# Two float16 parts of the normalised rows in the projection, and transposing DMAs for the experts' rows

## The chip, the cores and the metric

The kernel runs on one core of one Trainium2 chip. The metric is the device time of one execution in microseconds (us), lower is better. Five engines work side by side and meet at semaphores: PE (matmuls), ACT, DVE and POOL (elementwise work), and SP, which here does nothing but issue DMAs, in one order, from one queue. The kernel before takes 1036.85 us (median of 3 runs, 1036.43 to 1039.17).

## The reference, cut to what matters

```python
x = L0_attn_X                                   # (2, 2048, 256) float32
xn = (x - mean) / sqrt(var + 1e-5)              # layernorm over the last axis
qkv = xn @ Wqkv                                 # 16 heads of 16, rope on q and k
attn = softmax(causal(q @ k.T / 4)) @ v         # each head
out_a = attn @ Wout + bout
p = softmax(xn @ gate_w.T + gate_b)             # 8 experts and 2 null ones
w, e = top_k(p, 2)                              # null ones masked, the rest renormalised
out_f = sum_k w[k] * (xn @ expert_w[e[k]] + expert_b[e[k]])
return x + out_a + out_f
```

## The kernel before

Float32 products are made of float16 parts: a value is a high part plus a low part, and three float16 products (high by high, high by low, low by high) replace one float32 product. So everything that PE multiplies has to be split somewhere.

**Projection** (`project`, until about 135 us). 4096 rows are taken in 8 steps s of 512 rows (chunk j, batch b, s = 2j + b). In a step:
- DVE takes the statistics (L480, L484) and forms `rstd` and `less` (L489, L491).
- ACT writes the normalised rows to `xn` as float32 (`normal_x`, L405) for step s + 2, near the end of its step s.
- PE turns them by 8 transposes against a float32 identity into `psT` (`transposes`, L709). It does so for step s + 1 between the second and the third of a step's four `queries` products, and then computes `values` (L717).
- ACT copies `psT` to float16 as the high part (`high_x`, L388). DVE subtracts to get the low part (`low_x`, L498).
- DVE multiplies each product by the rope tables (`rope`, L559). POOL combines the halves (L356, L358). ACT and then POOL or DVE split the result (`high` L413, `low` L345, `split` L564).
- SP stores `xn` as float32 rows to `norm_scratch` (L257), and the parts of q, k and v.

ACT's order in a step matters below: `high(s-1, 2)`, `high(s-1, 3)`, `high_x(s+1)`, `high(s, 0)`, `high(s, 1)`, `copy_v`, `normal_x(s+2)`, `high_e(s)`. So the cast that POOL's second `low` of a step waits for stands behind the next `normal_x`.

**Attention and experts** (`attend`, about 135 to 1000 us). Eight groups g of four heads. What each engine does in a group is written out in a string, `PE_ORDER`: `s` is a score matmul, `p` the product of one block of probabilities with V, digits are matmuls for the row maxima (reduced on DVE), `m` and `o` small transposes, `x` and `y` expert work. All engines walk the same string, each doing its own share in that order. Items other than `s` and `p` take turns in the two slots of `psP`.

Groups 2 to 5 are of the kind "experts". The token rows, sorted by expert, form 36 pairs of 128-row tiles, 9 per group. For pair n:
- POOL fetches its rows by indirect DMA (`fetch`, L1130) and splits them into float16 parts (`split`, L1141 and L1143).
- `x`: PE turns them by 8 transposes (`turn_x`, L1478). ACT copies the high half (L1231), DVE the low half (L1303) to `xT`.
- `y`: PE multiplies by the experts' weights (`expert`, 12 matmuls of 256 columns at L1494 and two for the bias at L1496). ACT copies the result out (L1234). SP waits for that copy, stores it (`store_e`, L1050) and loads the weights of pair n + 2 (`load_e`, two register reads of the expert's number and four DMAs, L1044 and L1046).

Between these, SP also issues the loads of heads for group g + 2 (L74, 24 DMAs, and L1027) and the small stores of row maxima (`store_m`, L1038), each at its place in the same order.

**Output** (`output`, the last 40 us): transposes, the Wout product and the sums.

Of the kernel before, what the change touches and what calls it, by code (L numbers as in the profile page):

```python
# [27 lines left out]
P = 128  # L28
# [29 lines left out]
ONE = 1  # L58
# [23 lines left out]
def project(nc, x, wqk, wvg, we, be, bout, gb, cos, sin, qk_s, v_s, we_s, be_s, xd, ys, acc, xn, escale, idx, unscale, etab, bo,  # L82
            hot, ge, eye, later, identf, identh, lane, number, at, Qs, Ks):
    with ExitStack() as ctx:
# [36 lines left out]
        less = [sb(f"less{i}", [P, CT]) for i in range(2)]  # L121
        vst = [sb(f"vst{i}", [P, CT, HEADS, VW]) for i in range(2)]
# [24 lines left out]
        past = sb("past", [P, MTILES, EXPERTS])  # L147
# [15 lines left out]
        xn_ok = sem("xn_ok")  # L163
# [37 lines left out]
        tables = sem("tables")  # L201

# [9 lines left out]
        def _(sp):  # L212
# [61 lines left out]
        def _(pool):  # L274
# [3 lines left out]

            def step(ins):
                steps[0] += 1  # L280
                return ins.then_inc(pool_step, 1)

            def stepped():
# [7 lines left out]
                                    pattern=[[-1, P]], channel_multiplier=1).then_inc(const, 1)  # L291
            for b in range(NB):
                nc.gpsimd.memset(vst[b][:, :, :, :], 1.0).then_inc(const, 1)
# [25 lines left out]
            pool.sem_inc(const, 1)  # L319

# [3 lines left out]
            nc.gpsimd.memset(identh[:, :], 0.0).then_inc(pool_b, 1)  # L324
            pool.wait_ge(pool_b, ONE + 4)
# [11 lines left out]
            for unit in (identf, identh):  # L337
                nc.gpsimd.affine_select(out=unit[:, :], in_=unit[:, :], compare_op=ALU.not_equal, fill=1.0, base=0,
                                        pattern=[[-1, P]], channel_multiplier=1).then_inc(const_b, 1)
            pool.wait_ge(const_b, ONE + 4 * SIDES + 2)  # L340
# [6 lines left out]
            def body(j):  # L347
                if j == 1:
                    pool.wait_ge(trig_in[1], ONE + 32)
                for b in range(NB):  # L350
                    s = 2 * j + b
                    for k0 in range(0, QKT, 2):
# [7 lines left out]
                        low(s, k0)  # L360

# [17 lines left out]
        def _(act):  # L379
# [21 lines left out]
            def normal_x(s, j, b):  # L401
                act.wait_ge(less_ok, ONE + s + 1)
                for t in range(CT):
# [1328 lines left out]
```

## Time and profile before

| | us |
|---|---|
| median of 3 runs | 1036.85 |
| span of the profiled execution | 1039.8 |
| projection, 0 to 135 | 135 |
| groups 0 and 1, 135 to 366 | 231 |
| groups 2 to 5, with the experts, 366 to 813 | 447 |
| groups 6 and 7, 813 to 1000 | 187 |
| output | 39.8 |

| engine | busy us, share of the span |
|---|---|
| PE | 926.0 (89%) |
| DVE | 863.4 (83%) |
| ACT | 714.7 (69%) |
| POOL | 462.6 (44%) |

The profile is of one execution; its span is 3 us above the median of the runs. A row of the timeline gives the start, the duration, the engine, the line and the tiles, and in brackets how long the engine sat idle before it and what ended that. Rows for `SPq` are the issuing of a DMA by SP, not the transfer. All tiles of the experts' stage are cut from one big tensor, so the trace calls each of them `xn`.

### The profile page before, as it was taken

To read this page: it belongs to the slowest core of one execution; us is meant where nothing else is said; L and a number is where in the kernel's file an instruction comes from. 1 tells how busy PE (TensorE), PEld (TensorE's weight loads), DVE (VectorE), ACT (ScalarE), POOL (GpSimd) and SP (SyncE) were. 2 spreads that over 40 slices of the span, in tenths; PEclk is the share of its full clock that TensorE was granted. 3 is DMA by queue.
4 is the path that set the end of the run, shared out by engine and by line. 5 is a ranking of instruction groups with operands and counts; after the bars stand their busy time and mean duration, and the time that the engine had idled before them with its cause. 6 is when DMAs were issued, how large, how long until landed. Compare 5 with 4: busy or idle time off the path is not lost. (4 is left out here: it accounts for less than half of the span.)

```text
span 1039.8 us, 22117 instructions
## 1 busy us (share of the span) xinstructions
PE 926.0 (89%) x7874; PEld 388.5 (37%) x7874; DVE 863.4 (83%) x1132; ACT 714.7 (69%) x1542; POOL 462.6 (44%) x588
## 2 busy tenths in 40 slices
PE   3888446999999999999999999999999799999978
PEld 1554312232433334344434433344334333333257
DVE  6999789899899977987797787878797599995856
ACT  3556201788788777876787677867887588789922
POOL 4677568565102234253814564262422255345510
PEclk9999655999999999999999999999999899999989
DMA  9767710301100334054314442255514322012113
GB/s 322 267 240 270 244 44 17 96 3 52 53 2 21 94 113 124 26 155 141 110 42 132 122 136 82 62 155 134 123 34 132 87 58 62 22 57 63 47 41 122
DMA packets 82085, 106.65 MB, mean 103 GB/s; under 512 B 10000, under 2 KB 59064, under 8 KB 80952
## 3 DMA queue, kind: packets, MB, share of 16 engines
q1 hardware_dynamic: 74488, 85.83, 26.0%
q0 software_dynamic: 6528, 17.83, 6.7%
q10 hardware_dynamic: 960, 1.57, 0.5%
q8 instruction: 64, 1.05, 0.4%
q14 instruction: 45, 0.37, 0.1%
HBM read 67.37 MB, written 37.50 MB: 101 GB/s over the span
## 5 line engine op out<-in xcount | busy, mean ns | idle before, releaser
L1268 DVE TENSOR_REDUCE blk<-psP 128x2 f32<-128x1024 f32 (+2 forms) x576 | 639.9, 1161 | 103.5 <-PE psP L1422 43.8
L1213 ACT ACTIVATE probs<-psS 128x512 f32<-128x512 f32 (+3 forms) x1280 | 588.5, 541 | 194.0 <-PE psS L1462 174.4
L1462 PE MATMUL psS<-Qs,Ks 50*128 50x512 f16 (+3 forms) x1280 | 322.8, 355 | 12.6 <-ACT probs L1213 9.2
L1422 PE MATMUL psP<-Ks,Qs 48*128 48x512 f16 (+3 forms) x1280 | 284.2, 365 | 34.8 <-DVE blk L1268 21.9
L1517 PE MATMUL psO<-probs,Vs 128*32 128x512 f32 (+3 forms) x2560 | 305.3, 553 | 10.0 <-POOL probs L1107 8.9
L1107 POOL TENSOR_SCALAR_AFFINE_SELECT probs<-probs 128x512 f32<-128x512 f32 x128 | 88.1, 688 | 356.6 <-ACT probs L1213 341.0
L1462 PEld LDWEIGHTS psS<-Qs,Ks 50*128 50x128 f16 x1280 | 92.8, 94 | 241.8 <-ACT probs L1213 149.1
L1422 PEld LDWEIGHTS psP<-Ks,Qs 48*128 48x128 f16 x1280 | 75.5, 95 | 151.4 <-DVE blk L1268 100.7
L1425 PE MATMUL psP<-later,eye 64*128 64x128 bf16 x1024 | 90.3, 223 | 0.0
L1517 PEld LDWEIGHTS psO<-probs,Vs 128*32 128x32 f32 x2560 | 52.4, 109 | 92.1 <-issue 68.8
L1130 POOL DMA_INDIRECT xn<-norm_scratch,ids x72 | 69.4, 963 | 20.7 <-issue 11.4
L1425 PEld LDWEIGHTS psP<-later,eye 64*128 64x128 bf16 x1024 | 71.8, 99 | 16.4 <-issue 2.1
L1122 POOL TENSOR_SCALAR xn<-lane,at 128x128 f16<-128x128 f32 x64 | 38.5, 601 | 44.9 <-ACT probs L1213 23.8
L1494 PE MATMUL psP<-xn 128*128 128x256 f16 x432 | 57.4, 273 | 0.8 <-DVE xn L1303 0.8
L717 PE MATMUL psQ<-xp,wqp 128*128 128x512 f16 x192 | 47.3, 393 | 10.6 <-DVE turn L559 6.1
L1117 POOL DMA_INDIRECT xn<-expert_scratch,idx x32 | 30.3, 946 | 39.8 <-ACT probs L1213 21.0
L1494 PEld LDWEIGHTS psP<-xn 128*128 128x128 f16 x432 | 39.3, 98 | 21.6 <-DVE blk L1268 9.9
L1143 POOL TENSOR_TENSOR xn<-xn 128x512 f16<-128x512 f32 x36 | 41.6, 1155 | 3.0
L559 DVE TENSOR_TENSOR turn<-psQ,trig 128x1024 f32<-128x1024 f32 x32 | 38.4, 1218 | 2.6 <-DVE part L564 1.8
L1234 ACT COPY xn<-psP 128x512 f32<-128x512 f32 x36 | 21.1, 585 | 26.9 <-PE psP L1496 26.9
L1125 POOL TENSOR_SCALAR xn<-lane,at,number 128x76 f16<-128x76 f32 x64 | 39.3, 614 | 0.0
L356 POOL TENSOR_TENSOR turn<-turn 128x512 f32<-128x512 f32 x16 | 24.0, 1500 | 23.0 <-DVE turn L559 22.7
(171 smaller groups left out, 744.0 us busy)
## 6 DMA issues: line engine op xcount, KB each, us to landing
xn<-we_scratch SPq DMA_DIRECT2D x72, 256.0 KB
expert_scratch<-xn SPq DMA_DIRECT2D x36, 256.0 KB
v_scratch<-vst SPq DMA_DIRECT2D x8, 1024.0 KB, 4.0
qk_scratch<-part SPq DMA_DIRECT2D x32, 256.0 KB, 4.0
Vs<-v_scratch SPq DMA_DIRECT2D x16, 512.0 KB, 4.3
Qs<-qk_scratch SPq DMA_DIRECT2D x168, 32.0 KB
Ks<-qk_scratch SPq DMA_DIRECT2D x168, 32.0 KB
acc<-x SPq DMA_DIRECT2D x8, 512.0 KB, 9.1
```

Of the source, the lines that this page charges most:

```text
L717: ins = pe.matmul(out, lhs(x, w, k), rhs(x, w, k), start=(n == 0), stop=(n == len(todo) - 1))
L1107: nc.gpsimd.affine_select(out=v, in_=v, compare_op=ALU.is_ge, fill=0.0, base=0, pattern=[[0, HG], [1, P]], channel_multiplier=-1).then_inc ...
L1125: nc.gpsimd.tensor_scalar(at_tile[:, n, :], lane[:, 0:MTILES], at[:, 0, n:n + 1], number[:, t:t + 1], ALU.is_equal, ALU.mult).then_inc(lis ...
L1130: nc.gpsimd.indirect_dma_start(out=xt[n % 2][:, t, :], out_offset=None, in_=xd[:, :], in_offset=bass.IndirectOffsetOnAxis(ap=ids[:, 2 * n ...
L1143: nc.gpsimd.tensor_tensor(xs[n % 2][:, 1, :], rows, xs[n % 2][:, 0, :], ALU.subtract).then_inc(x_split, 1)
L1213: nc.scalar.activation(probs[u % NPR][:, h, q0:CH], psS[:, n % SB, q0:CH], ACT.Exp, scale=exp_scale).then_inc(s_read[n % SB], 1)
L1268: nc.vector.tensor_reduce(out, src, AX.X, ALU.max).then_inc(item_ok[slot], 1)
L1422: ins = pe.matmul(psP[:, slot, at:at + w], Qs[r][rows, qt // CT, p, t * P:(t + 1) * P], Ks[r][rows, kc, p, 0:w], start=True, stop=True)
L1425: ins = pe.matmul(psP[:, slot, at + w - P:at + w], eye[all_rows, i, :], later[all_rows, i, :], start=False, stop=True, skip_group_check=True)
L1462: pe.matmul(psS[:, n % SB, q0:CH], Ks[r][rows, kt // CT, p, kt % CT * P:(kt % CT + 1) * P], Qs[r][rows, c, p, q0:CH], start=True, stop=Tru ...
L1494: pe.matmul(psP[:, slot, t * D:(t + 1) * D], xT[buf][:, w0, at_k:at_k + P], wt[2 * buf + t][:, of:of + D], start=(n == 0), stop=False)
L1517: ins = pe.matmul(psO[h * VW:(h + 1) * VW, q0:CH], Vs[r][:, kt, h * VW:(h + 1) * VW], probs[u % NPR][:, h, q0:CH], start=(kt == 0), stop=e ...
```

## The change

In the projection the normalised rows go to a float32 buffer `xf`; ACT casts them to the high part, POOL subtracts to get the low part (`low_rows`), and both lie side by side in `xrows`, in the place of `xn`. PE turns the float16 parts, 16 transposes for 8; ACT and DVE copy one half of `psT` each. The scratch holds both parts, 1024 bytes a row as before. In the experts' stage POOL no longer splits, PE no longer turns; SP issues two transposing DMAs a pair (`turn_x`) behind the store and the loads of the pair before. `x` is struck from the order, and nothing else in it is moved. `fetch(n+2)` now waits on POOL for the turning of pair n.

```diff
+            def low_rows(s):
+                j, b = divmod(s, NB)
+                of = slice(b * TT + j * CT, b * TT + (j + 1) * CT)
+                pool.wait_ge(rh_ok, ONE + s + 1)
+                nc.gpsimd.tensor_tensor(xrows[:, of, 1, :], xf[b][:, :, :], xrows[:, of, 0, :], ALU.subtract).then_inc(rl_ok, 1)
...
+            low_rows(0)
+            low_rows(1)
...
                         low(s, k0)
+                    if s + 2 < NB * CHUNKS:
+                        low_rows(s + 2)
...
             def high_x(s, b):
-                for k in range(KC):
-                    act.wait_ge(xT_ps, ONE + KC * s + k + 1)
-                    nc.scalar.copy(xp[b][:, 0, k, :], psT[:, k, :]).then_inc(xh_ok, 1)
+                act.wait_ge(xT_ps, ONE + 2 * s + 1)
+                nc.scalar.copy(xp[b][:, 0, :, :].rearrange("p k n -> p (k n)"), psT[:, 0, :].bitcast(F16)).then_inc(xh_ok, 1)
...
             def normal_x(s, j, b):
...
-                    ins = nc.scalar.activation(xn[:, tile, :], acc[:, tile, :], ACT.Identity, bias=less[b][:, t:t + 1],
+                    ins = nc.scalar.activation(xf[b][:, t, :], acc[:, tile, :], ACT.Identity, bias=less[b][:, t:t + 1],
                                                scale=rstd[b][:, t:t + 1])
-                ins.then_inc(xn_ok, 1)
+                ins.then_inc(xf_ok, 1)
+                act.wait_ge(xf_ok, ONE + s + 1)
+                nc.scalar.copy(xrows[:, j * CT + b * TT:(j + 1) * CT + b * TT, 0, :], xf[b][:, :, :]).then_inc(rh_ok, 1)
...
             def low_x(s, b):
-                for k in range(KC):
-                    dve.wait_ge(xh_ok, ONE + KC * s + k + 1)
-                    nc.vector.tensor_tensor(xp[b][:, 1, k, :], psT[:, k, :], xp[b][:, 0, k, :], ALU.subtract
-                                            ).then_inc(xl_ok, 1)
+                dve.wait_ge(xT_ps, ONE + 2 * s + 2)
+                nc.vector.tensor_copy(xp[b][:, 1, :, :].rearrange("p k n -> p (k n)"), psT[:, 1, :].bitcast(F16)
+                                      ).then_inc(xl_ok, 1)
...
             def transposes(s, j, b):
-                pe.wait_ge(xn_ok, ONE + s + 1)
-                pe.wait_ge(xl_ok, ONE + KC * s)
-                for k in range(KC):
-                    for t in range(CT):
-                        ins = pe.transpose(psT[:, k, t * P:(t + 1) * P], xn[:, j * CT + b * TT + t, k * P:(k + 1) * P],
-                                           ident[:, :])
+                pe.wait_ge(rl_ok, ONE + s + 1)
+                pe.wait_ge(xh_ok, ONE + s)
+                pe.wait_ge(xl_ok, ONE + s)
+                for w in range(2):
+                    for k in range(KC):
+                        for t in range(CT):
+                            ins = pe.transpose(psT[:, w, :].bitcast(F16)[:, k * CH + t * P:k * CH + (t + 1) * P],
+                                               xrows[:, j * CT + b * TT + t, w, k * P:(k + 1) * P], identh[:, :])
                     ins.then_inc(xT_ps, 1)
...
+            def turn_x(n):
+                sp.wait_ge(x_got[n % 2], 16 * 2 * (n // 2 + 1))
+                for t in range(2):
+                    sp.dma_start_transpose(xT[n % 2].rearrange("p w (k t n) -> p (w k) t n", k=KC, t=2)[:, :, t, :],
+                                           xt[n % 2][:, t, :]).then_inc(x_turned[n % 2], 16)
...
                         store_e(buf, EG * (g - 2) + x[1])
                         if EG * (g - 2) + x[1] + 2 < MTILES_USED // 2:
                             load_e(buf, EG * (g - 2) + x[1] + 2)
+                        if EG * (g - 2) + x[1] + 1 < MTILES_USED // 2:
+                            turn_x(EG * (g - 2) + x[1] + 1)
...
-            def split(n):
-                pool.wait_ge(x_got[n % 2], 16 * 2 * (n // 2 + 1))
...
-                    elif x[0] == "x":
+                    elif x[0] == "y":
                         n = EG * (g - 2) + x[1]
-                        turned[n] = slot_of(m), uses(g, m)
-                        if n + 1 < MTILES_USED // 2:
-                            split(n + 1)
+                        if n + 2 < MTILES_USED // 2:
+                            pool.wait_ge(x_turned[n % 2], 16 * 2 * (n // 2 + 1))
+                            fetch(n + 2)
...
                         elif x[0] == "y":
                             buf, before = pair_of(g, x[1])
+                            pe.wait_ge(x_turned[buf], 16 * 2 * (before + 1))
                             pe.wait_ge(e_in[buf], ONE + 16 * LOADS_E * (before + 1))
```

On ACT, in the projection, from one `normal_x` to the `high_x` after it, this stands before:

```order
L405 ACTIVATE xn<-acc,less,rstd 128x256 x4
L437 ACTIVATE wep<-we_sb,wscale 128x512
L413 CAST part<-turn 128x512 x2
L388 CAST xp<-psT 128x512 x2
L413 CAST part<-turn 128x512
```

and this now:

```order
L427 ACTIVATE xf<-acc,less,rstd 128x256 x4
L431 CAST xn<-xf 128x4x256
L461 ACTIVATE wep<-we_sb,wscale 128x512
L437 CAST part<-turn 128x512 x2
L407 COPY xp<-psT 128x1024
L437 CAST part<-turn 128x512
```

The cast of 1024 elements is new, ahead of the casts of `part` that POOL waits for; two copies have become one.

On POOL, one step of the projection now (L374 and L376 are the sums, L363 is `low`, L291 is `low_rows`):

```order
L374 TENSOR_TENSOR turn<-turn 128x512
L376 TENSOR_TENSOR turn<-turn 128x512
L363 TENSOR_TENSOR part<-turn,part 128x512
L374 TENSOR_TENSOR turn<-turn 128x512
L376 TENSOR_TENSOR turn<-turn 128x512
L363 TENSOR_TENSOR part<-turn,part 128x512
L291 TENSOR_TENSOR xn<-xf,xn 128x4x256
```

Before, the same six rows stood there without the seventh. It stands behind the second `low`.

On SP, in group 2, from the last load of one pair to the store of the next (pairs 4 and 5), with the loads of heads between, now:

```order
L1066 TENSOR_LOAD etab
L1066 ISA x2
L1067 ISA
L1067 DMA xn<-we_scratch 128x1024
L1069 ISA
L1069 DMA xn<-be_scratch 3x256
L1076 DMA_TRANSPOSE xn<-xn 128x4x128 x2
L74 DMA Qs0<-qk_scratch 8x2x1024 x12
L74 DMA Ks0<-qk_scratch 8x2x1024 x12
L1050 DMA Vs0<-v_scratch 128x8x128
L1080 DMA expert_scratch<-xn 128x2x256
```

The row L1076 is new. It turns pair 5, and the turning of pair 6 stands behind everything that is shown below it and the loads after that.

## Rows read from the trace of the kernel before

**Rows 1.** Windows by stage: us, busy per engine (instructions), PEclk, DMA share, GB/s.

```profile
0.00:135.00 135.00, 85.03 (x522) 52.12 (x522) 114.33 (x208) 62.50 (x126) 83.34 (x90) 0.92 0.74 259
272.00:366.00 94.00, 90.56 (x866) 32.67 (x864) 86.05 (x103) 75.06 (x165) 18.99 (x28) 1.00 0.17 48
...
366.00:813.00 447.00, 428.01 (x3932) 178.16 (x3931) 361.78 (x420) 339.87 (x726) 185.81 (x231) 0.99 0.37 106
```

**Rows 2.** Timeline of one projection step: start, duration, engine, line.

```profile
57.54 2.07 ACT L405 ACTIVATE xn<-acc,less,rstd 128x256 f32<-128x256 f32 x4
...
59.50 0.71 ACT L437 ACTIVATE wep<-we_sb,wscale 128x512 f16<-128x512 f32 x1
59.66 1.09 PE L709 MATMUL psT<-ident,xn 128*128 128x128 f32 x8 [1.10 <-ACT xn L405]
60.12 1.13 ACT L413 CAST part<-turn 128x512 f16<-128x512 f32 x2
60.59 2.75 PE L717 MATMUL psQ<-xp,wqp 128*128 128x512 f16 x12
60.80 1.16 POOL L345 TENSOR_TENSOR part<-turn,part 128x512 f16<-128x512 f32 x1 [0.65 <-ACT part L413]
...
62.44 1.28 DVE L498 TENSOR_TENSOR xp<-psT,xp 128x512 f16<-128x512 f32 x2
...
63.63 1.21 DVE L559 TENSOR_TENSOR turn<-psQ,trig 128x1024 f32<-128x1024 f32 x1
...
68.94 1.58 ACT L405 ACTIVATE xn<-acc,less,rstd 128x256 f32<-128x256 f32 x3
```

**Rows 3.** Groups of instructions by shape: busy us, mean ns | idle before.

```profile
L1143 POOL TENSOR_TENSOR xn<-xn 128x512 f16<-128x512 f32 x36 | 41.6, 1155 | 3.0
...
L1478 PE MATMUL psP<-identh,xn 128*128 128x128 f16 x288 | 22.4, 221 | 3.1 <-DVE blk L1268 2.1 <-ACT xn L1234 0.3 <-issue 0.3
...
L421 ACT ACTIVATE wqp<-wqk_sb,wscale 128x1024 f16<-128x1024 f32 x1 | 1.1, 1147 | 1.1 <-DVE wscale L512 1.1
```

**Rows 4.** Timeline of PE, ACT and SP around the first pairs of group 2.

```profile
377.11 0.83 PE L1494 MATMUL psP<-xn 128*128 128x256 f16 x6
...
378.85 0.59 ACT L1234 COPY xn<-psP 128x512 f32<-128x512 f32 x1 [0.91 <-PE psP L1496]
391.46 0.59 ACT L1234 COPY xn<-psP 128x512 f32<-128x512 f32 x1 [0.71 <-PE psP L1496]
398.57 0.58 ACT L1234 COPY xn<-psP 128x512 f32<-128x512 f32 x1 [0.80 <-PE psP L1496]
405.96 0.58 ACT L1234 COPY xn<-psP 128x512 f32<-128x512 f32 x1 [0.83 <-PE psP L1496]
...
383.36 0.31 SPq L1046 DMA_DIRECT2D xn<-be_scratch  x1
```

**Rows 5.** Timeline of SP and ACT around pairs 4 to 6 of group 2.

```profile
443.58 4.05 SPq L74 DMA_DIRECT2D Qs<-qk_scratch  x12
...
457.42 0.30 SPq L1046 DMA_DIRECT2D xn<-be_scratch  x1
...
445.61 0.58 ACT L1234 COPY xn<-psP 128x512 f32<-128x512 f32 x1 [0.77 <-PE psP L1496]
457.32 0.58 ACT L1234 COPY xn<-psP 128x512 f32<-128x512 f32 x1 [0.53 <-PE psP L1496]
```

**Rows 6.** DMA issues: tiles, engine, count, KB each, median us from issue to landing.

```profile
qk_scratch<-part SPq DMA_DIRECT2D x32, 256.0 KB, 4.0
...
we_scratch<-wep SPq DMA_DIRECT2D x8, 256.0 KB, 2.2
...
trig<-sin SPq DMA_DIRECT2D x1, 768.0 KB, 9.8
```

**Rows 7.** Windows on PE around its long idle stretch: us, busy (instructions), PEclk.

```profile
108.00:110.00 2.00, 0.59 (x6) 1.00 0.61 215
110.00:112.00 2.00, 0.00 (x0) 0.71 1.04 366
```

More of the change, by code:

```diff
@@ L121, in project @@
         less = [sb(f"less{i}", [P, CT]) for i in range(2)]
+        xf = [sb(f"xf{i}", [P, CT, D]) for i in range(2)]
+        xrows = xn[:, :, :].rearrange("p t d -> p (t d)").bitcast(F16).rearrange("p (t w d) -> p t w d", w=2, d=D)
         vst = [sb(f"vst{i}", [P, CT, HEADS, VW]) for i in range(2)]
@@ L201, in project @@
         tables = sem("tables")
+        unit = sem("unit")
         WQ = 6
@@ L806, in attend @@
         ids = sb("ids", [P, MTILES], U32)
-        xs = [flat[:, (11 + i) * CH:(12 + i) * CH].bitcast(F16).rearrange("p (w n) -> p w n", w=2) for i in range(2)]
         bt = [flat[:, 10 * CH + i * D:10 * CH + (i + 1) * D] for i in range(2)]
@@ L954, in order_of @@
                 queue.append(("m", 0, 1))
-            order, ns, nv, half, pairs = [], SB, 0, None, dict(x=0, y=0, r=0)
+            order, ns, nv, half, pairs = [], SB, 0, None, dict(y=0, r=0)
             outs = [("o", 0, c) for c in WALK]
@@ L974, in order_of @@
             assert not queue and not outs and nv == NU and ns == NU * HG + (SB if more else 0)
-            assert kind != "experts" or pairs == dict(x=EG, y=EG, r=0)
+            assert kind != "experts" or pairs == dict(y=EG, r=0)
             return order
@@ L985, in is_item, with slot_of @@
             x = order[at]
-            return x[0] in "moxyr" or x[0] == "q" and any(y[:-1] == x[:-1] for y in order[:at])
+            return x[0] in "moyr" or x[0] == "q" and any(y[:-1] == x[:-1] for y in order[:at])
         lists = {kind: [x for at, x in enumerate(orders[kind]) if is_item(orders[kind], at)] for kind in KINDS}
         NI = {kind: len(lists[kind]) for kind in KINDS}
-        assert all(NI[kind] % 2 == 0 for kind in ("plain", "route", "experts"))
         M_PARTS = {(0, 2): 2, (0, 1): 3, (1, 3): 4, (1, 0): 5}
         M_TURN = {(0, 0): 1, (0, 2): 2, (0, 1): 3, (1, 3): 4}
-        def slot_of(n):
-            return (NF + n) % 2
-        BEFORE = [sum(NI[kind] // 2 for kind in KIND[:g]) for g in range(GROUPS)]
+        BEFORE = [NF + sum(NI[kind] for kind in KIND[:g]) for g in range(GROUPS)]
+        def slot_of(g, n):
+            return (BEFORE[g] + n) % 2
         def uses(g, n):
-            return BEFORE[g] + (NF + n) // 2
+            return (BEFORE[g] + n) // 2
         def pair_of(g, i):
@@ L1093, in _ @@
                                 load_e(i, i)
+                            turn_x(0)
                     n += is_item(order, at)
@@ L1163, in _ @@
                     pool.wait_ge(pv_ok, PV0 + NU * g)
-                order, m = orders[KIND[g]], 0
-                for at_x, x in enumerate([("s", 0, i) for i in range(SB)] + order):
+                order = orders[KIND[g]]
+                for x in [("s", 0, i) for i in range(SB)] + order:
                     if x[0] == "s" and x[2] == HG - 1 and x[1] < NU:
@@ L1389, in _ @@
                         if not any(x[0] == "q" and (x[1], x[2] // CT) == key for x in items[n + 1:]):
-                            lasts = [max(k for k in range(n + 1) if items[k][0] == "q" and slot_of(k) == s)
+                            lasts = [max(k for k in range(n + 1) if items[k][0] == "q" and slot_of(g, k) == s)
                                      for s in range(2)]
-                            parts(4 * g + M_PARTS[key], key[1], [(slot_of(k), uses(g, k)) for k in lasts])
+                            parts(4 * g + M_PARTS[key], key[1], [(slot_of(g, k), uses(g, k)) for k in lasts])
                     elif item[0] == "m":
```

116 lines of the change are left out of this document (40 added, 76 removed).

## The prediction

> **What bounds the kernel now.** I read the table of stages first. The four groups with the experts take 447 us, and PE is busy in 428 of them, 96%; a plain group takes 94 us with PE busy in 90.6 [rows 1]. An expert group lasts 447 / 4 = 111.8 us, so 9 pairs cost 17.8 us, 1.97 us a pair. That is what PE's own work on a pair comes to: from the first expert matmul at 377.11 to the copy of its result at 378.85 are 1.74 us [rows 4], of which some 1.5 occupy PE, and the eight transposes take 22.4 us in 36 pairs, 0.62 each; one alone is 0.22, so they follow each other at (0.62 - 0.22) / 7 = 0.057 and occupy PE for some 0.5 [rows 3]. So the experts' stage is bound by PE, and removing work from PE there is worth its time if nothing else comes late.
>
> The projection is read from the timeline of a step. It repeats every 68.94 - 57.54 = 11.40 us [rows 2], with DVE busy in 114 of the 135 us [rows 1]. The loop that closes in one step runs: `normal_x` on ACT (2.07), transposes on PE (1.09, PE had waited 1.10 for it), the copy of the high part, the low part on DVE (62.44, ends at 63.72), `rope` for the third product at 63.63, then statistics and so to the next `normal_x` at 68.94, 5.3 us after that `rope` began. DVE is full all along, and this loop is about as long as DVE's work: there is no slack in it.
>
> **The experts' stage, what goes.** 36 times eight transposes leave PE: 36 x 0.5 = 18 us gained. POOL's split (L1143 alone 41.6 us [rows 3]) and the copies on DVE and ACT go too; none of the three is the bound, so they count nothing.
>
> **The experts' stage, what comes.** `turn_x(n+1)` stands on SP behind the wait for the result of pair n, its store, and the loads for pair n + 2. PE cannot begin pair n + 1 before it has landed, and on PE everything behind that `y` (scores, products with V, row maxima) waits as well. This makes a loop of pair n to pair n + 1:
> - copy of the result begins, until SP has issued the last load: 383.36 + 0.31 - 378.85 = 4.82 us [rows 4].
> - two transposing DMAs of 128 KB: no row shows one. Issuing a plain one costs SP 0.3 to 0.5 each, so 0.9 for two. From issue to landing the nearest rows are 2.2 us (256 KB, `we_scratch`) and 4.0 us (256 KB, `qk_scratch`) [rows 6]. I take 4.0, since two are in flight and SP's other transfers run beside them: 4.9 together. Lower bound 0.9 + 2.2 = 3.1; upper bound 0.9 + 9.8 = 10.7, the longest landing that the trace has.
> - expert matmuls to the next copy: 1.74.
>
> Sum 11.5 us (9.7 to 17.3). The order leaves less than that between many pairs. There are 36 such copies (L1234). In group 2 they begin at 378.85, 391.46, 398.57, 405.96 [rows 4], 438.15, 445.61, 457.32 [rows 5], 465.90 and 478.19, and group 3 begins with 490.33; the other groups lie within a microsecond or so of this. The gaps are 12.6, 7.1, 7.4, 32.2, 7.5, 11.7, 8.6, 12.3 and 12.1, each 0.5 shorter once the transposes are gone. Stalls of PE:
> - 7.1: 11.5 - 6.6 = 4.9. 7.4: 4.6. 7.5: 4.5. 8.6: 3.4. Together 17.4.
> - 11.7, pairs 5 to 6: SP issues the loads of heads from 443.58 on, and only then the store and the loads of pair 5, the last of them at 457.42, already after the copy of pair 6 at 457.32 [rows 5]. Only then could pair 6 be turned: 457.7 + 4.9 + 1.7 = 464.3 for its copy, about 7 late against 457.3 - 0.5. Of these 4.5 have been paid at pair 5, since a late pair 5 finds SP as far behind: 2.7 more.
> - 12.1, last pair to the next group's first: the loads of heads are issued there too, for 8.7 us: 6.5, three times in all.
> - 12.6, 12.3 and 32.2: nothing.
>
> Sum (17.4 + 2.7) x 4 + 6.5 x 3 = 100 us. Less the 18 that PE gains: +82. With 3.1 instead of 4.9 for the DMAs the same sum gives about +47, with 10.7 about +230.
>
> POOL now waits at `y` for the turning of its pair before it fetches pair n + 2. Behind it on POOL are the masks of later units, which PE has not reached by then, so nothing. The row maxima's stores on SP come about 1 us later behind two more issues; I cost them at nothing (at most 1 us each for 16 of them, if PE reached the chunk at once).
>
> The Trainium skill speaks on both ends here. "Advanced Engine Details and Errata", X-Bar Transpose (TRN2), says that such DMAs are as fast as regular ones; by that the sum above stands. "VectorE: DVE Perf Modes", The three transpose paths, gives 1309 ns for a 128x128 tile by DMA; a pair has eight, which one after another would be an estimated 10.5 us and the rival below. The traces of this kernel have no transposing DMA and decide nothing between them.
>
> **The projection, what comes.** Between `normal_x` and the transposes now stand, in this order: ACT's cast of 1024 elements (1.15, as L421 [rows 3]), `high_e` (0.71) and the cast for `low` (half of 1.13), since POOL's `low_rows` is behind `low` in its order and `low` behind that cast; `low` (1.16) [rows 2]; `low_rows`, twice the 1.155 of a subtraction of 512 elements [rows 3], 2.3; and hand-overs, some 0.3. From 57.54: 2.07 + 1.15 + 0.71 + 0.57 + 1.16 + 2.3 + 0.3 = 8.3, so the transposes begin at 65.8 instead of 59.66. They are 16 at the 0.057 worked out above, 0.9 and the end of the last, so I keep 1.09. The third `queries` product is half of 2.75 behind them, and `rope` can begin at 65.8 + 1.1 + 1.4 = 68.3 instead of 63.63: +4.7 us a step. DVE's `low_x`, one copy now for 1.28 us of subtractions, is hidden in it. Steps 0 to 5 pass through this loop (`normal_x` of step s + 2): 6 x 4.7 = +28. At the start the two first `low_rows` fall while POOL and PE wait for data and weights: nothing. Bounds: 4 us a step with quick hand-overs, 24; 7 us with the clock below, 43.
>
> **The clock.** After PE's last matmul at 108.6 the granted clock is still 1.00 until 110 and on average 0.71 in the two us after it, so it falls to its half, 1.2 GHz, within about 2.3 us of idleness [rows 7]. In the projection PE will now sit idle for 65.8 - 58.6 = 7.2 us in each step, and in the experts' stage for 3 to 7 us some 23 times. Matmuls run at half speed for a while after such a wait. In a projection step transposes and one product, 2.5 us at full speed, lie on the loop; I count half of that, 1.2 x 6 = 7. For the 23 stalls I count 0.5 us each, 11.
>
> **Sum.** On the profiled execution, 1039.8 - 18 + 100 + 28 + 7 + 11 = 1168; that execution lies 3 us above the median of the runs, so 1165.
>
> **Rivals.**
> - *PE's gain alone.* If the turned rows always lay ready, and the projection absorbed its longer loop, the 18 us would show: 1037 - 18 = 1019. For it speaks that PE is the bound at 96%. Against it: it needs a loop of at most 6.6 us from pair to pair, and 4.82 + 1.74 = 6.56 are used before the DMAs have taken any time at all; and DVE in the projection has no slack. This is the side on which I would be wrong in sign, from 0.1 us for both DMAs.
> - *The transposing DMA is slow.* With landings as long as the longest of the trace the loop is 17.3 us, every gap but the 32 us one stalls, and the sum is 1037 + 230 + 43 + 15 = 1325. The skill's figure per tile would put it here. For it: it is another kind of transfer than any in the trace. Against it: nothing in the trace.
> - *Short DMAs and a cheap projection.* 3.1 us for the DMAs, 4 us a step, no loss by the clock: 1037 + 47 + 24 = 1108. For it: the 2.2 us row, and SP's queue is light in many of these stretches.
>
> **How the numbers follow.** Forecast 0.68, slow DMA 0.15, short DMAs 0.13, PE's gain alone 0.03, an exact balance 0.01. The measurement of this kernel tells about 0.3% from no change. All cases but the last two are slower by far: slower 0.96, same 0.01, faster 0.03. The range reaches from a little under the short case, 1095, to 1265, where the two DMAs take 8 us together (+160 net in the experts' stage, 43 in the projection, 25 by the clock); what is left out above is the slow case at its full price.
>
> **What would show it.** In the profile after: in the experts' groups PE idle, ended by a DMA, before L1483, some 20 times; the copies of results at least 11 us apart; groups 2 to 5 of some 133 us. In the projection a step of about 16 us, with DVE waiting for PE's transposes and PE for POOL's L291. If the expert groups are near 112 us the loop argument is wrong; if the step stays at 11.4 us, the second loop is.

## The result, and the profile after

The changed kernel takes 1169.09 us (median of 4 runs, 1165.45 to 1173.57) against 1037.86 us for the kernel before on the same chip (4 runs, 1036.43 to 1039.17): ratio 1.1266, 95% interval 1.1234 to 1.1299. It is slower by 131 us; a time of 1165 us was forecast. The profiled execution has a span of 1166.1 us (before 1039.8).

Windows by stage of the kernel after (us; busy us and instructions of PE, PE's weight loads, DVE, ACT, POOL; granted clock; DMA share; GB/s), answering to [rows 1]; the groups with the experts now lie between 402 and 941:

```profile
0.00:135.00 135.00, 75.62 (x441) 45.47 (x442) 83.39 (x153) 61.64 (x110) 79.40 (x84) 0.83 0.57 202
270.00:366.00 96.00, 93.62 (x888) 33.38 (x889) 89.73 (x104) 78.37 (x171) 22.90 (x38) 1.00 0.10 29
402.00:941.00 539.00, 444.45 (x3654) 174.04 (x3648) 346.24 (x385) 321.88 (x690) 127.59 (x164) 0.90 0.39 105
```

The end of a group is taken where DVE begins its last reciprocal of row sums (L1288, before L1277). The first group ends at 309.4 us instead of 271.8: the projection costs 37.6. Groups 2 to 5 take 538.6 instead of 447: 91.6 more. By the spans, everything else together is 3 us shorter. In the experts' window PE is idle for 539 - 444.45 = 94.6 us, where it was idle for 19.0.

Lines of the page of the kernel after (busy us, mean ns, idle before and its releaser), its packets, and from its DMA table the landing:

```profile
DMA packets 121249, 116.05 MB, mean 100 GB/s; under 512 B 49168, under 2 KB 98232, under 8 KB 120120
...
L1483 PE MATMUL psP<-xn 128*128 128x256 f16 x432 | 77.7, 334 | 81.7 <-issue 81.7
...
L1163 POOL DMA_INDIRECT xn<-norm_scratch,ids x72 | 68.5, 951 | 114.4 <-DMA xn<-xn 101.6
...
L743 PE MATMUL psQ<-xp,wqp 128*128 128x512 f16 x192 | 53.6, 437 | 3.2 <-DVE xp L521 3.0
...
L735 PE MATMUL psT<-identh,xn 128*128 128x128 f16 x128 | 14.2, 300 | 41.9 <-POOL xn L291 40.6
```

```profile
xn<-xn SPq DMA_TRANSPOSE x72, 2.7
```

Two lines carry most of the loss: PE waits 81.7 us before the experts' first matmul and 40.6 us before the transposes of the projection. The first is put down to "issue"; the timeline below shows that what it waits for are SP's transposing DMAs, and POOL's wait of 101.6 us, for the same transfers, names them.

Waits of PE between 402 and 941, kernel after (total us, times, longest):

```profile
PE psP L1483 <- issue: 81.7, 25, 7.6
PE psS L1464 <- ACT probs L1227: 4.3, 18, 0.9
PE psP L1424 <- DVE blk L1279: 3.6, 15, 0.4
```

**One turn of the experts' loop.** Timeline of ACT, SP and PE in the kernel after, from the copy of one pair's result to the next (start, duration, engine, line):

```profile
424.65 0.59 ACT L1245 COPY xn<-psP 128x512 f32<-128x512 f32 x1 [0.71 <-PE psP L1485]
...
425.35 0.41 SPq L1080 DMA_DIRECT2D expert_scratch<-xn  x1
426.75 0.32 SPq L1067 DMA_DIRECT2D xn<-we_scratch  x1
...
429.08 0.31 SPq L1069 DMA_DIRECT2D xn<-be_scratch  x1
429.44 2.53 SPq L1076 DMA_TRANSPOSE xn<-xn  x2
...
433.34 0.82 PE L1483 MATMUL psP<-xn 128*128 128x256 f16 x6 [3.56 <-issue]
...
434.10 1.40 PE L1483 MATMUL psP<-xn 128*128 128x256 f16 x6
...
435.75 0.58 ACT L1245 COPY xn<-psP 128x512 f32<-128x512 f32 x1 [6.03 <-PE psP L1485]
```

Copy, store, loads, two transposing DMAs, matmuls, next copy: 11.1 us, where the order had left 7.1 between the same two copies. The second six matmuls take 1.40 instead of 0.82. The granted clock shows when it fell; two windows of the same turn, one in PE's wait and one from 0.7 us behind its end:

```profile
430.00:433.00 3.00, 0.00 (x0) 0.00 (x0) 0.04 (x1) 0.00 (x0) 0.00 (x0) 1.00 0.61 156
434.00:437.00 3.00, 3.00 (x19) 1.42 (x20) 0.28 (x1) 1.25 (x3) 1.40 (x2) 0.53 0.30 85
```

So PE sat idle for 3.6 us at a granted clock of 1.00, worked for about 0.8 us more at it, and then had 0.50, 1.2 GHz, for some 3 us. Not every wait does this. Of the 24 waits of over 0.5 us before L1483, 17 were followed within a microsecond, or already at their end, by 0.50; one began at 0.50; six (of 1.1 to 3.5 us) left the clock at 1.00 for the next 5 us.

**One step of the projection.** Timeline of ACT, POOL, PE and DVE in the kernel after:

```profile
70.72 2.07 ACT L427 ACTIVATE xf<-acc,less,rstd 128x256 f32<-128x256 f32 x4
...
72.82 1.04 ACT L431 CAST xn<-xf 128x1024 f16<-128x1024 f32 x1
73.77 0.72 ACT L461 ACTIVATE wep<-we_sb,wscale 128x512 f16<-128x512 f32 x1
74.39 1.12 ACT L437 CAST part<-turn 128x512 f16<-128x512 f32 x2
75.07 1.15 POOL L363 TENSOR_TENSOR part<-turn,part 128x512 f16<-128x512 f32 x1 [1.75 <-ACT part L437]
...
76.18 2.57 POOL L291 TENSOR_TENSOR xn<-xf,xn 128x1024 f16<-128x1024 f32 x1
...
78.81 1.89 PE L735 MATMUL psT<-identh,xn 128*128 128x128 f16 x16 [6.73 <-POOL xn L291]
...
80.49 3.81 PE L743 MATMUL psQ<-xp,wqp 128*128 128x512 f16 x12
80.73 0.69 DVE L521 COPY xp<-psT 128x1024 f16<-128x1024 f16 x1 [3.96 <-PE psT L735]
...
83.18 1.23 DVE L582 TENSOR_TENSOR turn<-psQ,trig 128x1024 f32<-128x1024 f32 x1 [1.75 <-PE psQ L743]
```

The chain runs through ACT's cast, `high_e`, the casts that `low` waits for, `low`, `low_rows`, and PE starts 8.1 us behind `normal_x` (2.1 before, [rows 2]). PE's granted clock is 0.50 from before its start until about 82.3, so all the transposes and most of the product run at half speed (1.89 and 3.81, before 1.09 and 2.75). The step is 18.0 us (`normal_x` at 52.68, 70.72 and 88.67; the last two are 17.3); it was 11.4.

### The profile page after: what moved, and what is told of

Its sections match the earlier page's. It is cut to its first block and busy times, and to the rows that moved or that the text cites. A ratio compares the mean times of both kernels' runs of the same rounds, so it can differ in the third digit from the quotient of the medians.

```text
span 1166.1 us, 21559 instructions
## 1 busy us (share of the span) xinstructions
PE 948.7 (81%) x7650; PEld 390.1 (33%) x7650; DVE 844.8 (72%) x1088; ACT 705.1 (60%) x1506; POOL 412.5 (35%) x524
## 2 busy tenths in 40 slices
DMA packets 121249, 116.05 MB, mean 100 GB/s; under 512 B 49168, under 2 KB 98232, under 8 KB 120120
## 5 line engine op out<-in xcount | busy, mean ns | idle before, releaser
L1464 PE MATMUL psS<-Qs,Ks 50*128 50x512 f16 (+3 forms) x1280 | 331.3, 360 | 14.1 <-ACT probs L1227 9.1
L1424 PE MATMUL psP<-Ks,Qs 48*128 48x512 f16 (+3 forms) x1280 | 293.1, 371 | 33.0 <-DVE blk L1279 21.0
L1506 PE MATMUL psO<-probs,Vs 128*32 128x512 f32 (+3 forms) x2560 | 305.7, 553 | 10.4 <-POOL probs L1140 8.5
L1464 PEld LDWEIGHTS psS<-Qs,Ks 50*128 50x128 f16 x1280 | 94.8, 95 | 253.6 <-ACT probs L1227 158.5
L1483 PE MATMUL psP<-xn 128*128 128x256 f16 x432 | 77.7, 334 | 81.7 <-issue 81.7
L1424 PEld LDWEIGHTS psP<-Ks,Qs 48*128 48x128 f16 x1280 | 76.1, 95 | 146.6 <-DVE blk L1279 92.1
L1163 POOL DMA_INDIRECT xn<-norm_scratch,ids x72 | 68.5, 951 | 114.4 <-DMA xn<-xn 101.6
L1245 ACT COPY xn<-psP 128x512 f32<-128x512 f32 x36 | 21.1, 585 | 135.6 <-PE psP L1485 119.5
L1483 PEld LDWEIGHTS psP<-xn 128*128 128x128 f16 x432 | 47.3, 116 | 111.3 <-issue 94.3
L743 PE MATMUL psQ<-xp,wqp 128*128 128x512 f16 x192 | 53.6, 437 | 3.2 <-DVE xp L521 3.0
L582 DVE TENSOR_TENSOR turn<-psQ,trig 128x1024 f32<-128x1024 f32 x32 | 38.5, 1222 | 15.3 <-PE psQ L743 12.7
L735 PE MATMUL psT<-identh,xn 128*128 128x128 f16 x128 | 14.2, 300 | 41.9 <-POOL xn L291 40.6
L374 POOL TENSOR_TENSOR turn<-turn 128x512 f32<-128x512 f32 x16 | 21.6, 1353 | 33.3 <-DVE turn L582 32.8
```

The source lines that it names most:

```text
L582: nc.vector.tensor_tensor(turn[k][:, :, :], psQ[:, k % 2, :].unsqueeze(1).to_broadcast([P, 2, CH]), trig[:, :, bass.ds(j * CH, CH)], ALU.m ...
L743: ins = pe.matmul(out, lhs(x, w, k), rhs(x, w, k), start=(n == 0), stop=(n == len(todo) - 1))
L1163: nc.gpsimd.indirect_dma_start(out=xt[n % 2][:, t, :], out_offset=None, in_=xd[:, :], in_offset=bass.IndirectOffsetOnAxis(ap=ids[:, 2 * n ...
L1424: ins = pe.matmul(psP[:, slot, at:at + w], Qs[r][rows, qt // CT, p, t * P:(t + 1) * P], Ks[r][rows, kc, p, 0:w], start=True, stop=True)
L1464: pe.matmul(psS[:, n % SB, q0:CH], Ks[r][rows, kt // CT, p, kt % CT * P:(kt % CT + 1) * P], Qs[r][rows, c, p, q0:CH], start=True, stop=Tru ...
L1483: pe.matmul(psP[:, slot, t * D:(t + 1) * D], xT[buf][:, w0, at_k:at_k + P], wt[2 * buf + t][:, of:of + D], start=(n == 0), stop=False)
```

## The experiments

Each kernel was timed against the kernel before on the same chip. That one took 1033.3 to 1041.2 us from chip to chip, so kernels are compared by their ratio and by the length of their stages. The lengths are those of the one profiled execution.

**1. The projection alone.** The changed projection; the fetched float16 rows are again turned by PE, at the old places of `x` in the order, and neither SP nor a DMA turns anything.

```diff
-            def turn_x(n):
-                sp.wait_ge(x_got[n % 2], 16 * 2 * (n // 2 + 1))
-                for t in range(2):
-                    sp.dma_start_transpose(...)
+            def turn_x(g, x, slot):
...
+                pe.wait_ge(x_got[buf], 16 * 2 * (before + 1))
+                for w in range(2):
...
+                            ins = pe.transpose(psP[:, slot, :].bitcast(F16)[:, at_k:at_k + P],
+                                               xt[buf][:, t, w * D + k * P:w * D + (k + 1) * P], identh[:, :])
```

> The projection's part of the change alone: rows split there, fetched as float16 parts and turned by PE with the order of before, no transposing DMA. Theory of two loops: the projection keeps its longer step (18.0 us against 11.4, six times, about +37 in all), the experts' groups fall back to some 447 us; 1037 + 37 = 1074 us. Rival (what the experts' stage lost is not the turning's wait but the transfers and the weaker clock around it, which here stay away as well) gives the same number; rival that the projection costs little: 1045 or less.

Measured 1080.95 us (1078.86 to 1081.38), ratio 1.0435 (1.0409 to 1.0462). The first group ends at 309.65, groups 2 to 5 take 448 us. Window of that kernel:

```profile
402.00:850.00 448.00, 432.34 (x3944) 179.02 (x3944) 359.70 (x421) 339.19 (x726) 127.93 (x164) 0.99 0.36 106
```

By the medians this is 44 us above the kernel before on the same chip, where 37 was expected; by the profiled spans (1077.1 and 1039.8) it is 37.3. The profile of the kernel before is of an execution 3 us above its median. So the +37.6 are the projection's, to within these few us, and the experts' stage is at its old length although POOL no longer splits (127.9 us of work instead of 185.8): POOL's work there was worth nothing, as forecast.

**2. The experts alone.** The projection of before with float32 rows, POOL's split, and transposing DMAs in the experts' stage.

```diff
-                pe.wait_ge(rl_ok, ONE + s + 1)
+                pe.wait_ge(xn_ok, ONE + s + 1)
...
+            def split(n):
+                pool.wait_ge(x_got[n % 2], 16 * 2 * (n // 2 + 1))
...
+                nc.gpsimd.tensor_copy(parts[:, :, 0, :], xt[n % 2][:, :, :]).then_inc(x_high, 1)
...
+                nc.gpsimd.tensor_tensor(parts[:, :, 1, :], xt[n % 2][:, :, :], parts[:, :, 0, :], ALU.subtract).then_inc(x_split, 1)
```

> The experts' part alone: projection of before with float32 rows, POOL splits the fetched rows as before and SP turns them by transposing DMAs. Theory: the loop from one pair to the next through SP costs what it costs in the changed kernel, groups 2 to 5 near 539 us; 1038 + 92 = 1130 us. Rival (the two parts make each other worse): under 1115.

Measured 1137.07 us (1131.93 to 1140.19), ratio 1.0965 (1.0920 to 1.1010). The first group ends at 272.0, as before; groups 2 to 5 take 546.6. The costs are apart by stage: +38 there, +92 to +100 here. In this kernel the stage is 8 us longer than in the changed one. PE's busy time in it is the same (443.5 and 444.3 us), and 7.4 of the 8 us are longer waits before the experts' matmuls:

```profile
PE psP L1472 <- issue: 89.1, 25, 6.0
```

The split on POOL, which stands ahead of the turning here, is what differs; that it makes these waits longer is not shown.

**3. Turning before the wait.** Two kernels open the experts' loop. In the first, SP turns pair n + 1 before it waits for the result of pair n. In the second it does so behind the store but ahead of the loads.

```diff
                         buf, _ = pair_of(g, x[1])
+                        if EG * (g - 2) + x[1] + 1 < MTILES_USED // 2:
+                            turn_x(EG * (g - 2) + x[1] + 1)      # first kernel
                         sp.wait_ge(item_ok[slot_of(g, n)], ONE + uses(g, n) + 1)
...
                         store_e(buf, EG * (g - 2) + x[1])
+                        if EG * (g - 2) + x[1] + 1 < MTILES_USED // 2:
+                            turn_x(EG * (g - 2) + x[1] + 1)      # second kernel
                         if EG * (g - 2) + x[1] + 2 < MTILES_USED // 2:
                             load_e(buf, EG * (g - 2) + x[1] + 2)
-                        if EG * (g - 2) + x[1] + 1 < MTILES_USED // 2:
-                            turn_x(EG * (g - 2) + x[1] + 1)
```

> The changed kernel with one edit: SP issues the turning of pair n + 1 ahead of its wait for the result of pair n. Theory: the loop is opened, PE finds the rows turned, the stalls of some 5 a group go, and PE's 18 us show: groups 2 to 5 at 429 to 440 us, in all 1169 - 105 = 1064 us (1055 to 1075). Rival (the transposing DMA itself is too slow, or takes bandwidth from the loads that PE needs): 1130 or more.

> The changed kernel with the turning of pair n + 1 issued behind the store of pair n but ahead of its four loads. Theory: the loop is 3.7 us shorter, about 7.4 us instead of 11.1; by the gaps between pairs of the kernel before, PE then waits some 32 us in all (most of it where the loads of heads stand between) and gains its 18: groups 2 to 5 at 447 + 14 to 20 = 461 to 467 us, in all 1169 - 75 = 1094 us (1085 to 1103). Rival (any transposing DMA beside the loads is slow): no change from 1169.

Measured: first 1084.31 us (1081.65 to 1088.44), ratio 1.0473 (1.0434 to 1.0513), groups 2 to 5 in 451.8 us; second 1114.36 (1107.28 to 1122.39), ratio 1.0775 (1.0701 to 1.0848), 477.6 us. The order of a few lines on SP is thus worth 87 of the 92 us, and two thirds of it come already when the 4 us of loads leave the loop. That the place of `turn_x` in SP's order makes the loss is shown. But neither number came. The second was expected at 1094, with 32 us of waits; PE waits 46.0 us there, 15 times. The first was expected at 1064, with PE's 18 us as a gain. The first kernel's window, its waits before L1483, and SP and PE at one of them:

```profile
402.00:854.00 452.00, 415.64 (x3655) 165.38 (x3655) 346.16 (x387) 320.81 (x690) 128.03 (x164) 0.97 0.49 125
```

```profile
PE psP L1483 <- issue: 23.3, 8, 4.7
```

```profile
509.59 4.22 SPq L74 DMA_DIRECT2D Qs<-qk_scratch  x12
513.85 4.06 SPq L74 DMA_DIRECT2D Ks<-qk_scratch  x12
517.96 0.39 SPq L1050 DMA_DIRECT2D Vs<-v_scratch  x1
518.39 2.57 SPq L1076 DMA_TRANSPOSE xn<-xn  x2
...
522.84 0.82 PE L1483 MATMUL psP<-xn 128*128 128x256 f16 x6 [1.66 <-issue]
```

PE's work did shrink, from 428 to 416 us, but it waits 23 us in eight places. At seven of them SP comes late from its 8.7 us of heads' loads.

**4. Every transposing DMA twice.** The first of each goes to an unused buffer.

```diff
                 for t in range(2):
+                    sp.dma_start_transpose(<unused buffer>, xt[n % 2][:, t, :]).then_inc(x_turned[n % 2], 16)
+                for t in range(2):
                     sp.dma_start_transpose(...)
```

> The changed kernel with every transposing DMA issued twice, the first time into a buffer that nothing reads. Theory (a loop from pair to pair, that SP's issuing is part of): two more issues of 1.27 us each make the loop 2.55 us longer, 13.7 us; by the gaps between the pairs of the kernel before PE waits some 67 us more: 1169 + 67 to 75 = about 1240 us. Rival (bandwidth: the data moved by them is what costs, 256 KB a pair): 1169 + 36 x 0.7 = 1195 us or less.

Measured 1259.60 us (1256.28 to 1268.29), ratio 1.2125 (1.2069 to 1.2181); groups 2 to 5 take 623.5. Waits of PE there:

```profile
PE psP L1486 <- issue: 149.1, 30, 8.6
```

84.9 us more in the stage, where some 70 were expected. PE starts 3.9 us behind the issue of the pair of DMAs that it needs, as in the changed kernel, and 6.5 behind the issue of the pair ahead of it (medians of 27 waits): the 2.55 us that two more DMAs hold SP are passed on in full. 67.4 of the 84.9 are longer waits (149.1 against 81.7), as the 67 expected; the rest came with more busy time of PE (463.3 against 444.3) at a slower clock (0.85 in the stage, 0.90 in the changed kernel). The loop is closed by SP. The rival of bandwidth alone, 1195 or less, has fallen.

**5. One transposing DMA a pair.** One of 128x8x128 instead of two of 128x4x128; the order of the turned blocks in `xT`, and PE's reads of it, follow.

```diff
-                for t in range(2):
-                    sp.dma_start_transpose(xT[n % 2].rearrange(...)[:, :, t, :], xt[n % 2][:, t, :]).then_inc(x_turned[n % 2], 16)
+                sp.dma_start_transpose(xT[n % 2].rearrange("p w n -> p (w n)").rearrange("p (c n) -> p c n", n=P),
+                                       xt[n % 2].rearrange("p t n -> p (t n)")).then_inc(x_turned[n % 2], 16)
```

> The changed kernel with one transposing DMA of 128x8x128 for a pair of blocks instead of two of 128x4x128; everything else stays. The theory says that the experts' groups 2 to 5 go round a loop on SP once in each of about 27 to 33 gaps, and that each DMA's 1.27 us on SP is in it. If SP pays that once an instruction, the loop is 1.27 us shorter and the time comes to about 1169 - 34 = 1135 us. Rival: SP pays by the block that is turned, so one DMA of double size holds it for about 2.5 us and the time stays at about 1169 us, or is a little longer, as the first half no longer lands ahead of the second.

Measured 1155.98 us (1152.70 to 1160.43), ratio 1.1193 (1.1157 to 1.1229), groups 2 to 5 in 529.1 us. Neither number came. SP and PE in its timeline, and the line of its DMA table:

```profile
429.59 1.29 SPq L1075 DMA_TRANSPOSE xn<-xn  x1
...
433.07 1.44 PE L1482 MATMUL psP<-xn 128*128 128x256 f16 x6 [3.15 <-issue]
```

```profile
xn<-xn SPq DMA_TRANSPOSE x36, 3.5
```

SP does pay by the instruction (1.29 for eight blocks, 2.53 for two times four), which the theory had right. But PE starts 3.48 us behind the start of the issue (433.07 - 429.59) instead of 3.90 (433.34 - 429.44): the larger transfer takes 3.5 us to land instead of 2.7, and the first of the two had been landing while SP issued the second. Over all waits of the stage the median is 3.6 us against 3.9. So of the 1.27 us only 0.3 to 0.4 leave the loop, and 9.5 us the stage.

**6. The projection's two parts.** One kernel keeps PE's clock up with 24 matmuls of 512 columns, whose result is overwritten, ahead of the wait for `low_rows`. The other puts `low_rows` ahead of the second `low` on POOL.

```diff
             def transposes(s, j, b):
-                pe.wait_ge(rl_ok, ONE + s + 1)
                 pe.wait_ge(xh_ok, ONE + s)
                 pe.wait_ge(xl_ok, ONE + s)
+                for _ in range(24 if s >= 2 else 0):
+                    pe.matmul(psT[:, 0, :], wqp[:, 0, 0, 0:P], xp[b ^ 1][:, 0, 0, :], start=True, stop=True)
+                pe.wait_ge(rl_ok, ONE + s + 1)
```

```diff
+                        if k0 == 2 and s + 2 < NB * CHUNKS:
+                            low_rows(s + 2)
                         low(s, k0)
-                    if s + 2 < NB * CHUNKS:
-                        low_rows(s + 2)
```

> The changed kernel, with 24 matmuls of 512 columns more on PE (results thrown away) in six steps of the projection, at the place where PE otherwise sits idle for 6.7 us until the low rows are there. Nothing else is changed. Theory (part of the longer step is PE at its lower clock after that wait): transposes to the rope of the third product take 2.5 us instead of 4.4, the step falls from 18.0 to 16.1 us, the whole by 6 x 1.9 = 11 us to 1158. Rival (the clock plays no part in the step): 1169, step 18.0.

> The changed kernel with POOL's low_rows of step s + 2 ahead of the second low of step s, not behind it. Theory (the order of POOL's queue, behind a cast on ACT that stands behind high_e, is part of the chain): low_rows can begin at the end of ACT's cast, 2.3 us earlier; step 15.7 us instead of 18.0, 1169 - 14 = 1155 us. Rival (POOL's amount of work sets the step, not its order): no change.

Measured: warm 1154.58 us (1153.79 to 1159.49), ratio 1.1167 (1.1150 to 1.1184), first group's end 300.4, step 16.0; other order 1153.63 (1151.33 to 1154.56), ratio 1.1163 (1.1146 to 1.1180), 293.7, step 15.2. PE in a step of the warm kernel, and POOL and PE in one of the other:

```profile
69.31 5.34 PE L732 MATMUL psT<-xp,wqp 128*128 128x512 f16 x24
...
76.44 1.07 PE L737 MATMUL psT<-identh,xn 128*128 128x128 f16 x16 [1.78 <-POOL xn L291]
77.34 2.75 PE L745 MATMUL psQ<-xp,wqp 128*128 128x512 f16 x12
```

```profile
67.09 1.04 ACT L431 CAST xn<-xf 128x1024 f16<-128x1024 f32 x1
68.22 2.12 POOL L291 TENSOR_TENSOR xn<-xf,xn 128x1024 f16<-128x1024 f32 x1 [0.62 <-ACT xn L431]
70.30 1.60 POOL L363 TENSOR_TENSOR part<-turn,part 128x512 f16<-128x512 f32 x1
70.40 1.53 PE L735 MATMUL psT<-identh,xn 128*128 128x128 f16 x16 [3.66 <-POOL xn L291]
```

Both are shown: the clock is worth 2.0 us of a step (transposes and product back at 1.07 and 2.75), the order on POOL 2.8. The first group ends 9.0 us earlier with the clock kept up, and not 6 x 2.0: in one of the six steps the clock fell even so, and the last two steps of the changed kernel were at 17.3 us already. The experts' stage stays within 4 us of its 538.6 in both (541.1 and 542.5).

**7. Where PE's 18 us stay.** If nothing comes late they should show. Four kernels turn rows a pair ahead, `turn_x(n + 2)` behind the loads of pair n, so that the loop has two gaps to close in. A keeps the changed projection and lets POOL fetch pair n + 3 at `y` n, behind the turning of pair n + 1; B is the same with the projection and the split of before. C and D are A and B with the fetch of pair n + 2 behind the turning of pair n, which is long done by then. The first turnings and fetches ahead of group 2 follow suit.

```diff
-                        if EG * (g - 2) + x[1] + 1 < MTILES_USED // 2:
-                            turn_x(EG * (g - 2) + x[1] + 1)
+                        if EG * (g - 2) + x[1] + 2 < MTILES_USED // 2:
+                            turn_x(EG * (g - 2) + x[1] + 2)
...
-                        if n + 2 < MTILES_USED // 2:
-                            pool.wait_ge(x_turned[n % 2], 16 * 2 * (n // 2 + 1))
-                            fetch(n + 2)
+                        if n + 3 < MTILES_USED // 2:
+                            pool.wait_ge(x_turned[(n + 1) % 2], 16 * 2 * ((n + 1) // 2 + 1))
+                            fetch(n + 3)
```

> The changed kernel with the turning of pair n + 2 behind the loads for pair n + 2, a whole pair ahead of its use, and POOL's fetches a pair earlier. Theory (in the run with the turning issued just ahead of the wait, the four groups took 451 us because SP came late behind the loads of heads): PE finds every pair turned, its waits before the expert matmuls go, PE's 18 us show: groups 2 to 5 at 430 to 437 us, in all 1169 - 105 = 1064 us. Rival (the 18 us cannot be had, since the waits of PE for ACT and DVE take their place): groups 447, in all 1077.

> The projection of the kernel before, POOL's split of the fetched rows, transposing DMAs for PE's transposes, each issued a whole pair ahead. If the 18 us of PE show: 1037 - 14 to 18 = 1019 to 1023 us, faster than both kernels. If other waits take their place: 1033 to 1040. Theory: the first, with 1023.

> As the kernel that turns a whole pair ahead (1077 us), but POOL fetches pair n + 2 at the result of pair n, behind a turning that is long done, so that POOL is not blocked ahead of its masks; SP may wait for the fetch instead. Theory (there POOL waited 85 us for turnings, and PE then for POOL's masks and for turned rows): groups 2 to 5 fall from 447 to some 436 us, in all 1066 us. Rival (the transposing DMAs hold back PE in another way, or ACT and DVE take over as the bound): 1075 to 1080.

> Projection of the kernel before, POOL's split, transposing DMAs a whole pair ahead, and POOL splits pair n + 2 at the result of pair n. Theory as for the last kernel: 1033 - 8 to 12 = 1021 to 1026 us, faster than both kernels. Rival (nothing of PE's 18 us can be had): 1033 to 1045.

| kernel | us, median (range) | ratio (interval) | groups 2 to 5, us |
|---|---|---|---|
| A | 1077.14 (1074.74 to 1088.86) | 1.0443 (1.0392 to 1.0494) | 447.0 |
| B | 1060.04 (1052.64 to 1064.79) | 1.0244 (1.0210 to 1.0278) | 473.3 |
| C | 1100.46 (1094.18 to 1110.40) | 1.0612 (1.0562 to 1.0662) | 459.6 |
| D | 1052.08 (1042.99 to 1058.49) | 1.0103 (1.0058 to 1.0149) | 464.8 |

The lengths are of the profiled execution, for C the fastest of four and for D the slowest of six. In A and C (and in experiment 4) PE waits once more, 2.2 to 2.6 us for row maxima, just ahead of what is counted here as the start of group 2. With that wait A takes 449.4 us and C 462. D is within 1.5% of the kernel before, the others are slower by more.

My theory of a gain fell four times. Window of A with that wait in it, PE's waits in it, and one of POOL's:

```profile
403.70:853.10 449.40, 416.55 (x3664) 166.44 (x3664) 346.27 (x386) 321.41 (x692) 125.29 (x162) 0.98 0.49 125
```

```profile
PE psP L1487 <- DMA xn<-xn: 8.4, 4, 2.5
PE psP L1428 <- DVE blk L1283: 5.4, 20, 0.7
PE psO L1510 <- POOL probs L1141: 5.4, 5, 1.7
PE psS L1468 <- ACT probs L1231: 5.2, 19, 0.8
PE psS L1468 <- DMA Qs<-nmT: 4.8, 4, 2.6
```

```profile
POOL xn L1164 <- DMA xn<-xn: 83.1, 19, 9.1
```

PE is busy for 11.5 us less than in [rows 1] and idle for 32.9 us instead of 19.0, so the stage keeps about its 447. The waits that were not there before are for turned rows (8.4), for POOL's masks (5.4, they stand behind its 83 us of waiting for turnings) and for row maxima stored late on SP (4.8). In B the masks alone cost PE 24.4 us of its stage. In C and D, where POOL waits little (8.5 and 12.7 us for turnings), PE waits 13.6 and 12.1 us for turned rows and 11.6 and 4.2 for row maxima. SP has one order for loads, stores, maxima and turnings, and each pair takes 2.55 us more of it. The DMA engines are also busy for more of the stage (0.49 of it in A, 0.37 before). What of these waits is SP's order and what is contention in the DMA engines was not separated. No kernel here beats the one before.

## Why the prediction was right, and where its parts were not

The forecast, 1165 (1095 to 1265), has the mechanism, both stages and the sum; of its terms several missed and cancelled. That the sum came within 4 us is in part luck: in the experts' stage the stalls were put 24 us too high and the price of the clock 23 us too low.

- *Experts' loop.* Forecast 11.5 us as 4.82 + 4.9 + 1.74; measured 4.74 (424.65 to 429.39) + 3.95 (to 433.34) + 2.41 (to 435.75) = 11.1. The DMAs' 4.9 were wrong twice: issuing two costs SP 2.53 us, not 0.9, and one lands in 2.7, not 4.0. The result's 1.74 had no slower clock in it.
- *Gap by gap.* From the starts of ACT's nine copies (L1245) in group 2 and the first of group 3:

| gap before | 12.6 | 7.1 | 7.4 | 32.2 | 7.5 | 11.7 | 8.6 | 12.3 | 12.1 |
|---|---|---|---|---|---|---|---|---|---|
| forecast | 12.1 | 11.5 | 11.5 | 31.7 | 11.5 | 13.9 | 11.5 | 11.8 | 18.1 |
| measured | 12.6 | 11.1 | 11.8 | 31.7 | 11.2 | 16.9 | 10.4 | 10.9 | 18.3 |

  They sum to 133.6 and 134.9. The others are within 1.1 us; the one miss is the sixth, where I took 4.5 us of SP's lateness behind the heads' loads as paid already. Without that the forecast would have been 18.4, so some 1.5 were. Group 3 takes 139.2 for its nine gaps, 18.5 in the sixth and 12.6 in the seventh place; group 4 takes 134.0.
- *Stalls and clock.* Forecast 100 us of stalls, 11 by the clock, 18 gained: +93. Measured +91.6, otherwise made up. PE's idle time grew by 94.6 - 19.0 = 75.6 us, and its busy time by 444.5 - 428.0 = 16.4, although 18 us of transposes had left (an estimate of the prediction; PE's busy time differs by 16.7 between experiment 1 and the first kernel of experiment 3): slower matmuls cost some 34. The experts' 432 alone rose from 57.4 to 77.7 us (273 to 334 ns). The step that missed is "0.5 us" for each stall: the 25 waits left the clock at 0.90 over the stage (0.99 before), about 1.4 us a wait. The prediction priced a short stretch of half speed behind every stall. In the trace six waits cost none, and the other stretches at 0.50 lasted about 3 us and more; in 6 of the 17 the clock fell only when PE was at work again. So other lines pay too, such as the scores (L1464, 168.5 us of the stage; 158.3 before) and the row maxima (L1424, 144.1; 134.6 before).
- *Projection.* The start of the transposes was forecast at +8.3 us behind `normal_x` and came at 8.1, with `low_rows` longer (2.57, not 2.3) and hand-overs shorter. The step became 18.0 instead of 16.1 + 1.2. The clock is the term that missed: 2.0 us a step (experiment 6), not 1.2. Taken together +37.6, where 28 + 7 = 35 was forecast.
- *Costed at nothing.* POOL's wait at `y` and the later maxima on SP cost nothing in the changed kernel: neither is among PE's waits between 402 and 941. In the kernels of experiment 7 they are part of what takes the gain (10.2 us of waits in A, beside 8.4 for turned rows). The forecast would have been wrong there.
- *The rivals.* PE's gain alone needed a loop of 6.6 us; no kernel here had it, and even with the loop opened the gain stayed out. The slow DMA fell: eight blocks of 128x128 were there 3.9 us after SP began to issue them. The Trainium skill gives 1309 ns for one 128x128 tile by DMA ("VectorE: DVE Perf Modes", The three transpose paths). The estimated 10.5 us for eight of them, one after another, is not what the trace shows. The Trainium skill also says that transpose DMAs are as fast as regular ones ("Advanced Engine Details and Errata", X-Bar Transpose (TRN2)). For the landing the traces agree (3.5 us for the 256 KB of experiment 5, beside 2.2 to 4.0 for plain DMAs of 256 KB, [rows 6]), for the issue they do not (1.27 us against 0.3 to 0.4).
- *Signs named ahead.* Some 20 waits before L1483: 25, and put down to "issue", not to a DMA. Groups of some 133 us: 134.7. A step of about 16: 18. PE waiting for L291: 40.6 us in 6 waits.

## What to carry to other kernels

Work taken from the engine that bounds a stage is worth something only if its replacement is off the loop from one result to the next. Write that loop down with every queue that it passes, and compare it with the gaps that the order leaves: here that gave the time of each of nine gaps but one to 1.1 us. Then add what waiting does to PE's clock; here that was a third of the loss in the experts' stage (34 of 110 us, before the 18 gained). And a queue that only issues DMAs is an engine with a load of its own: with 2.5 us of issue per pair on SP, PE's 18 us came back at none of the places in the order that were tried.

## What the hardware showed that I had not expected

- A transposing DMA holds SP for 1.27 us, whether it turns four or eight 128x128 blocks of float16 (1.29); plain ones take 0.3 to 0.4 in the same place. Landing takes 2.7 and 3.5 us.
- It moves small packets: the count under 512 B rose from 10000 to 49168, 544 for each of the 72 DMAs, and by 38016 = 36 x 1056 with one DMA of double size for a pair (experiment 5). The DMA engines' share of time went from 0.37 to 0.39 only because the experts' stage had grown: 0.37 of 447 us are 165, 0.39 of 539 are 210. In the kernels whose stage stays near 450 us (the first of experiment 3, and A) the share is 0.49.
- POOL's subtraction of 1024 elements shows 2.57 us behind `low` (1.15) and 2.12 ahead of it (1.60). Both orders give 3.72 for the two together.
- PE's granted clock need not fall while PE waits. Behind the wait of 3.6 us shown above it fell to 0.50 only when PE had worked again for 0.8 us; in the six waits of the projection, 6.2 to 7.0 us, it was at 0.50 before PE began.
